# TensorE signals once for three tiles in a two-layer graph kernel, with more slots for gathered rows and selection matrices

## What is computed

```python
# block 0: two relational graph convolutions, 8 relations
W = einsum('rb,bio->rio', coeff[l], basis[l])
msg = einsum('ni,rio->rno', h, W)[etype, src] * norm
h = segment_sum(msg, dst) + bias[l]      # relu after the first
...
x = layernorm(x + h)
# block 1: input product, three mean-aggregation layers, output product
agg = segment_sum(h[src], dst) / deg
h = relu(agg @ W_agg[l] + h @ W_self[l] + b_hid[l])
...
x = layernorm(x + h @ W_out + b_out)
```

## Time and profile before

| | |
|---|---|
| median of 3 runs | 2400.35 us (2400.32 to 2401.89) |
| profiled execution | 2404.79 us, its span 2403.0 us |
| PE busy | 1856.1 us (77%) |
| DVE busy | 1197.0 us (50%) |
| POOL busy | 1252.7 us (52%) |
| ACT busy | 409.2 us (17%) |
| mean granted TensorE clock | 0.857 |

### The profile page before, as it was taken

How to read it: one execution, slowest core, us unless ns; L and a number is a source line. 1 busy time by engine, 2 the same in 40 slices (tenths; PEclk the granted TensorE clock), 3 DMA queues, 4 the chain that set the end, 5 groups by cost and what they waited for, 6 DMA issues and landing times.

```text
span 2403.0 us, 30886 instructions
## 1 busy us (share of the span) xinstructions
PE 1856.1 (77%) x9415; PEld 1517.0 (63%) x9415; DVE 1197.0 (50%) x3965; ACT 409.2 (17%) x875; POOL 1252.7 (52%) x1294
## 2 busy tenths in 40 slices
PE   4678778778777777657777777777667679999997
PEld 2556556666666566546666666666556567777776
DVE  6656644444444444334555554553367843232355
ACT  2001111111111111101111111111101014633332
POOL 5766766666666666366666666666666640000000
PEclk9678888878878888878888888888888789999999
DMA  6333333333333333233333333334533320000011
GB/s 207 88 93 97 99 98 96 100 96 98 99 99 96 98 98 98 60 93 98 101 103 98 99 105 97 102 102 122 171 101 95 97 70 11 1 1 1 1 35 44
DMA packets 118623, 208.27 MB, mean 87 GB/s; under 512 B 53828, under 2 KB 74196, under 8 KB 118456
## 3 DMA queue, kind: packets, MB, share of 16 engines
q0 software_dynamic: 62016, 169.04, 24.9%
q1 hardware_dynamic: 48848, 26.08, 3.8%
q10 hardware_dynamic: 7592, 11.13, 1.4%
HBM read 189.01 MB, written 17.13 MB: 86 GB/s over the span
## 4 chain that ended last, share of the span: by engine, by line
PE 64%; issue 16%; DVE 10%; another core or an unknown queue 6%; DMA 2%; DVEq 1%; POOL 1%; ACT 0%; ACTq 0%; SPq 0%; POOLq 0%
PE bank L650 26%; PE bank L610 15%; PE bank L822 11%; PE bank L593 4%; DVE RY L463 3%; PE bank L839 2%; PE bank L767 2%; DVE RY L452 2%; PE bank L592 1%; DMA RX<-in_basis 1%; POOL RY L258 1%; DVE RY L392 1%; DVEq L326 1%; DVE RY L391 1%
## 5 line engine op out<-in xcount | busy, mean ns | idle before, releaser
L650 PE MATMUL bank<-RY 128*128 128x128 f32 x5160 | 885.6, 318 | 360.3 <-issue 304.1
L650 PEld LDWEIGHTS bank<-RY 128*128 128x128 f32 x5160 | 794.3, 227 | 463.0 <-issue 375.9
L463 DVE TENSOR_SCALAR RY<-iot,c,wgt 128x128 f32<-128x128 f32 x1290 | 451.5, 360 | 826.1 <-remote 475.8
L258 POOL DMA_INDIRECT RY<-in_x,si x645 | 636.9, 987 | 338.0 <-issue 160.2
L258 POOL DMA_INDIRECT RY<-H,si x645 | 615.5, 954 | 371.2 <-issue 161.9
L822 PE MATMUL bank<-Ar,hs 125*128 125x500 f32 x1200 | 305.8, 405 | 0.0
L822 PEld LDWEIGHTS bank<-Ar,hs 125*128 125x128 f32 x1200 | 225.7, 188 | 51.7 <-issue 9.2
L511 ACT CAST RY<-bank 128x320 uint8<-128x320 f32 x215 | 91.7, 426 | 967.7 <-remote 605.2
L610 PE MATMUL bank<-RY 128*128 128x256 f32 x704 | 218.2, 436 | 45.7 <-DVE RY L452 24.9
L610 PE MATMUL bank<-RX,RY 128*128 128x256 f32 x704 | 225.9, 452 | 34.7 <-issue 21.0
L593 PE MATMUL bank<-RY 128*128 128x320 bf16 x645 | 196.6, 341 | 32.5 <-issue 27.5
(11 more groups left out here) (102 smaller groups left out, 869.7 us busy)
## 6 DMA issues: line engine op xcount, KB each, us to landing
RY<-in_x,si POOLq DMA_INDIRECT x645
RY<-H,si POOLq DMA_INDIRECT x645
Ad<-RY SPq DMA_DIRECT2D x215, 40.0 KB
RX<-Ad ACTq DMA_DIRECT2D x20, 305.2 KB
RX<-in_basis ACTq DMA_DIRECT2D x2, 2048.0 KB, 32.7
H<-RY SPq DMA_DIRECT2D x22, 128.0 KB
RY<-in_x SPq DMA_DIRECT2D x22, 128.0 KB
X<-RY SPq DMA_DIRECT2D x22, 128.0 KB
```

Of the source, the lines that this page charges most:

```text
L258: e.indirect_dma_start(G[0:k, n % NG, :], None, table, bass.IndirectOffsetOnAxis(ap=si[0:k, t:t + 1], axis=0)).then_inc(s_land[n % NG], 16)
L463: e.tensor_scalar(S[:, v % NSS, :], iot[:, :], c2[:, u:u + 1], wgt[:, u:u + 1], ALU.is_equal, ALU.mult).then_inc(s_sel, 1)
L650: mm = e.matmul(bank[2 + wg % 3][:, c * 128:(c + 1) * 128], G[0:k, n % NG, c * 128:(c + 1) * 128], S[0:k, n % NSS, :], start=(i == 0), sto ...
```

## The change

TensorE signals `s_sum` once for a group of three tiles, behind its last matmul, and `s_cnt` once for a group of counts. All waits on the two count groups. `G` gets 21 slots, `S` 18, `Mr` and `Nr` 9, and the region that holds them grows from 20,480 to 21,792 words in a partition. The carry matmul of a group of counts is issued at the end of the group before, and carries that group's signal; `Mp` is built one tile earlier. The first 16 gathers are issued in the setup as before (`FIRST`).

```diff
-NG = 16
-NSL = 8
-NSS = 16
+NG = 21
+NSL = 9
+NSS = 18
...
-                if n >= NG:
-                    e.wait_ge(s_sum, n - NG + 1)
+                if n >= NG and (n - NG) % TA == 0:
+                    e.wait_ge(s_sum, (n - NG) // TA + 1)
...
-                if u >= NSL:
-                    e.wait_ge(s_cnt, u - NSL + 2)
-                if u % TA == 0 and u > 0:
-                    w = u // TA
+                if u >= NSL and u % TA == 0:
+                    e.wait_ge(s_cnt, (u - NSL) // TA + 1)
+                if u % TA == TA - 1 and u < T - 1:
+                    w = u // TA + 1
                     e.tensor_scalar(Mp[:, w % 4, :], iotN[:, 0:128], pd2[:, w:w + 1], None, ALU.is_equal)
...
-            e.wait_ge(s_sum, l * T + min(T, TA * w + TA))
+            e.wait_ge(s_sum, wg + 1)
...
-                    if v >= NSS:
-                        e.wait_ge(s_sum, v - NSS + 1)
+                    if v >= NSS and (v - NSS) % TA == 0:
+                        e.wait_ge(s_sum, (v - NSS) // TA + 1)
...
-            e.wait_ge(s_cnt, a + 1)
+            e.wait_ge(s_cnt, w + 1)
...
-            b = bank[5 + w % 3]
             k = edge_rows(a)
-            if i == 0:
-                if 0 < w < 3:
-                    e.wait_ge(s_w1c, w)
-                elif w > 0:
-                    e.wait_ge(s_aw8, w - 2)
             e.wait_ge(s_hot, a + 1)
-            if i == 0 and w > 0:
-                e.matmul(b[:, 0:NB], Mp[:, w % 4, :], Nr[:, (a - 1) % NSL, :], start=True, stop=False)
-            e.matmul(b[:, 0:NB], Mr[0:k, a % NSL, :], Nr[0:k, a % NSL, :], start=(a == 0), stop=(i == TA - 1)).then_inc(s_cnt, 1)
+            mm = e.matmul(bank[5 + w % 3][:, 0:NB], Mr[0:k, a % NSL, :], Nr[0:k, a % NSL, :], start=(a == 0), stop=(i == TA - 1))
+            if i == TA - 1 and a < T - 1:
+                if w < 2:
+                    e.wait_ge(s_w1c, w + 1)
+                else:
+                    e.wait_ge(s_aw8, w - 1)
+                mm = e.matmul(bank[5 + (w + 1) % 3][:, 0:NB], Mp[:, (w + 1) % 4, :], Nr[:, a % NSL, :], start=True, stop=False)
+            if i == TA - 1:
+                mm.then_inc(s_cnt, 1)
...
-                    if c == 1:
-                        mm.then_inc(s_sum, 1)
+            mm.then_inc(s_sum, 1)
```

More of the change, by code:

```diff
@@ L181, in program @@
         with ExitStack() as inner:
-            RY = inner.enter_context(nc.sbuf_tensor("RY", [128, 20480], F32))
+            RY = inner.enter_context(nc.sbuf_tensor("RY", [128, 21792], F32))
         (Mr, Nr, Aw8, Mp, G, S, W2, ZA, Ew, Pg, hw, h1w, xw, xT) = lay(
@@ L958, in act_mean_layers @@
             last = NW - 1
-            e.wait_ge(s_sum, 2 * T)
+            e.wait_ge(s_sum, 2 * NA)
             e.wait_ge(s_ad, 16 * NA)
```

## The result

The changed kernel takes 2405.86 us (median of 12 runs, 2401.48 to 2408.79). The kernel before, measured between its runs, takes 2401.47 us (median of 12, 2397.99 to 2405.68). The ratio is 1.0017, with a 95% interval of 1.0009 to 1.0025: nothing gained, if anything 4 us lost. The forecast was 2282 us. Between the two the sign is open, and the size is clear: within a quarter of a per cent of no change.

What follows compares the result with a forecast made beforehand. The bound was read as a closed loop of late TensorE signals, no free slot and POOL pauses. Savings of 57, 49, 6 and 6 us took 2404.8 to 2286.8, less 4.4 for the median: 2282 us, range 2150 to 2415.

Steps and rivals of the forecast that it cites:

- (3): Gather stage: each gather costs POOL's pace plus 1.42 / n us, n the gathers between two pauses; together 118 us saved.
- n = 12: Gathers POOL would issue between two pauses in the changed kernel, where it was 6.
- (1): TensorE's signals: per group of three tiles 5 become 1.67, waiters served sooner; by the skill's rule 34 us at most.
- (2): Slots: POOL may be 21 gathers past a reported group rather than 16, DVE 18 matrices; no gather gets faster.
- (4): DVE's wait at L463 for s_sum falls away on two of three tiles; shortens the same loop, not counted again.
- (5): Counts: the carry matmul moves to the end of the group before, one step earlier; zero.
- (6): Layout: RY grows by 1,312 words and no instruction is added; zero.
- (7): The 31.7 us pause between layers, the 100 us start and the 438 us after 1965 us stay.
- B: Rival: nothing changes, since TensorE's whole stream may be late; 2400 us or a little less; chance 0.10.
- A: Rival: POOL's pauses all but vanish, 263 us by POOL's pace, so 2137 us; chance 0.26.
- C: Rival: slower, as only whole groups count and some bursts shrink to three gathers; 2464 us; chance 0.13.
- D: Rival: only the serial price of signals goes; 2366 to 2400 us, about 2385; chance 0.09.

Runs made afterwards that it cites:

- e11_bf16: Kernel before with its sums reading G and S as bf16, half the TensorE instructions there, on a pausing chip: 2369.84 us against 2399.17, ratio 0.9881.
- e2_signals: Changed kernel with 15 slots for rows and 15 for selection matrices, so one signal per group alone: 2106.22 us against 2112.61 for the kernel before, 0.9975.
- e17_after: Changed kernel without an edit, on a non-pausing chip: 2100.15 us against 2111.58 for the kernel before, ratio 0.994.

## Why the prediction was wrong

**The step that failed is (3), "What a cycle becomes".** "Per gather it costs 1.27 (or 1.25) + 1.42 / n us": the formula takes the pause for a fixed cost of 1.42 us that longer bursts spread thinner. The evidence was three pauses of 1.65, 1.73 and 1.79 us in a row, and all three stood behind bursts of six. "Its length hardly varies" was true because the burst didn't vary. The same trace holds bursts of nine with 2.13 us of extra time, so the formula was refuted by the profile of before. With an extra that is proportional, about 0.237 us per gather, n drops out, and the 118 us with it. The formula took the pause for what slows the stage. It is what POOL does while TensorE, at 1.49 us per tile, catches up.

**n = 12** was wrong too: the bursts stayed mostly six and partly nine. That is the smaller error, since e11_bf16 has mostly nine and gains 1.2%, and the extra goes with n.

**(1) Signals and the closed loop** ("late signals, so no free slot, so a pause, so signals"). That signals are late was right, and by more than was read. "Nearly 3 us after the matmuls" took the twelve matmuls that end at 1201.31 for those that POOL and DVE stood for. Counted in the code, gather 778 at 1204.39 and the matrix at 1204.16 need the signal of tile 762, from the group before:

```profile
1195.15 2.32 PE L650 MATMUL bank<-RY 128*128 128x128 f32 x11 [0.75 <-issue]
```

The tile's last matmul ends at 1196.61, 7.8 us before the gather. What was wrong is that fewer signals would be served sooner: 860 + 430 fewer bought nothing on two pausing chips, where the median lateness of what POOL waits for stayed at 7.0 to 7.4 us. On a non-pausing one they bought 0.25% (e2_signals; the medians differ by 6.4 us). The sentence on the Trainium skill's rule ("TensorE: Matmul & The Clock Gate", "The cost: per-tile semaphore tail") gave it 34 us at most; the runs stay within that bound, and I had argued against it. The prediction's own test was that it is "wrong at the root" if TensorE's "issue" idle before L650 "stays near 304 us and grows in share". It is 283.7 us in one pair, a little less of the span, and rose from 265.2 to 287.6 in the other: near enough, without a steady growth. The number of signals was no lever; whether their lateness and TensorE's stops have one cause stays open.

**(2) Slots.** "It makes no gather faster" held. What I left out is that a lead is given back: POOL waits 4.3 us longer at layer 0's end, and at layer 1's end 9.1 us of lead come to nothing (the last gather starts 6.84 us earlier, the last sums 2.28 us later). Twelve slots in place of 16 are even a little better on a pausing chip, 0.997 [0.9958, 0.9982], and worse on the other, 1.002.

**(4) DVE.** Its waits before L463 fell by 70 us, and the pace stayed. **(5)** and **(6)**, put at zero, have no run of their own. **(7)**, "stay", held but for the 4.3 us.

**The rivals.** B, "nothing changes", came true in its number (2400 us) and mostly in its test ("bursts still of six"; 35 are of nine), and I gave it 0.10. Of its reason, TensorE's whole stream being late at matmuls that carry no signal, the idle time without a semaphore (152 of 271 us) bears out the first half; a number of instructions between two pauses goes with the length of the bursts and with the 62 above, but half of the instructions are worth only 1.2%. A's price of 263 us, worked out from POOL's own pace, is about right as the price of the pauses: where nothing pauses, the kernel *before* takes 2112 us, against A's 2137. Its mechanism did not happen. What takes the pauses away is another chip or moment, not this change. C didn't happen: there are 12 bursts of three, 13 before. D's sum of 2385 us is closest of the forecasts of a gain.

**What stays open.** The cause. Where gathers pause, something makes TensorE take 0.21 to 0.24 us more per tile than POOL's 1.255 us, holds its signals back by some 7 us and stops it ahead of matmuls that wait for nothing. It doesn't go with slots (12, 16, 21), with signals, with half of the bytes, and only slightly with TensorE's instructions. It is absent without gathers. Whether it goes with their number isn't shown, since the kernel with half of them ran only where nothing pauses; nor whether it is a shared resource or a price per gather. In the kernel before 479 of the 917 recorded updates of `s_sum` (gathers 150 to 1140) fall in the 15% of the time in which POOL pauses; but a pause also ends with such an update, so this doesn't say which brings about the other.

## What to carry to other kernels

Before a pause is divided by more work, find pauses behind bursts of different lengths in the trace: a pause that grows with its burst is the arrears of a rate, and here neither slots nor fewer signals bought it back. Count in the code which signal a wait needs before the last work seen ahead of it is taken for its cause; here that was a group of three tiles off. Deeper buffers only moved the lead of the producer, which was given back at each boundary where the consumer had to finish. Where a gather's issue was the pace, its number counted: half the rows per gather saved 2%, half the gathers 21%.

## What the runs showed of the hardware

- The same kernel takes 2112 us on some chips and 2383 to 2401 us on others. The difference is in the stage of gathers: 1.25 to 1.27 against 1.47 to 1.49 us per gather. From the last sums to the end it is 428 us on either (e17_after, after). Each chip was used once, so chip and moment aren't told apart.
- On the pausing kind TensorE stands idle without any event, 265 to 304 us in all before the matmuls of sums (before, after and their repeats); without gathers it is gone.
- There POOL and DVE go on a median of 6.4 to 7.4 us after the matmul whose signal they need (before, after and their repeats), and DVE never more than 62 TensorE instructions after it. Where nothing pauses, and without gathers, it is 0.04 us.
- An indirect gather costs POOL 0.95 us and 0.30 us to the next one for 128 rows, and about 0.03 us less for 64.
- One small memset and wait between two gathers adds about 0.13 us to a gather's 1.26, two of them 0.6 us.
